# The opening of a fused attention kernel: load order, useless products and the second group's transposes

## Chip, cores and metric

The kernel runs on one core of a Trainium2 chip. The metric is the device time of the core in microseconds, from the start of the program to its end; before the change it is 969.23 us (median of 3 runs, 967.59 to 970.59).

## The reference

Six stages work on x, 16 batches of 128 tokens with 256 features in float32, each adding its result to x. Only the first, an attention with low-rank (LoRA) updates of its four weights, is touched:

```python
def lora_linear(x, W, b, Bm, Am):
    out = jnp.einsum('bld,od->blo', x, W) + b
    upd = jnp.einsum('blr,or->blo', jnp.einsum('bld,rd->blr', x, Bm), Am)
    return out + SCALING * upd           # rank 16, SCALING = 0.5
q = _split(lora_linear(x, Wq, bq, Bq, Aq))      # 16 heads of 16; k and v alike
scores = jnp.einsum('bhqd,bhkd->bhqk', q, k) * SCALE
attn = jax.nn.softmax(scores, axis=-1)
out = jnp.einsum('bhqk,bhkd->bhqd', attn, v)
return lora_linear(out, Wo, bo, Bo, Ao)
...
x = x + _L0_attn_ref(_layernorm(x, axis=-1), ...)
```

Then follow a causal convolution stage, a mixture of low-rank experts, a wide attention, a linear attention and a mixture of experts.

## The kernel before

Each engine has a program of its own, written out by hand, and the programs meet at semaphores. One function, lora_attention, gives the programs of the five engines for the first stage: sync_program (SP, which only issues transfers), gpsimd_program, tensor_program, scalar_program and vector_program. The order of the work on each engine is the order of the lines.

The 16 batches are worked in NG = 4 groups of G = 4. The unit of the attention loop (n, from 0 to 63) is four heads of one batch, so that a group has U = 16 units; g and u are group and unit (lines 533 and 534). In unit n TensorE transposes the probabilities (turn), makes the scores of units n + 4 and n + 5 on even n (scores), multiplies the values of unit n - 1 (weigh), and projects a batch now and then (project). Between these, `extra` puts the next group's input through its steps: transposes of the normalised input (turn_x, chunk 0 and 1, line 178), products for queries and keys (q_or_k) and values. Each large product is made of three with high and low parts of the operands (lines 50 to 52). ScalarE makes the high parts (hi_chunk, line 185), keeps the queries, keys and values that come out of PSUM (keep_q, keep_k, keep_v) and takes the exponentials (exps). VectorE makes the low parts (lo_chunk, line 189), row maxima (row_max), inverse sums, and the copies of the transposed probabilities (keep_probT), and the layer norm (vector_stats, vector_apply). GpSimd takes the power for the norm (line 173) and normalises the probabilities (line 332).

Ahead of the loop comes the opening. SP loads the LoRA factors (lines 300 and 301), x of the first group in two halves (303), the queries' weight (305) and the other three (306), waits for six transfers (`loaded`), and then loads x of the other groups and what later stages need. ScalarE issues five small transfers on its own queue: the unit matrix ident, then v_bias, out_bias, qk_bias and parity (559 to 563). TensorE waits for the factors (494), multiplies each weight's factors (503), then runs eight products whose result nobody reads (keep_busy, 498) on the factors' own tiles, waits for `loaded`, transposes the first group's input, runs three more useless products, and goes on with queries, keys, the bias product (521), the scores of units 0 to 3, the values, and the transposes of chunk 0 of group 1 (530). VectorE adds the factor products to the raw weights (fold, 726), ScalarE rounds them (637) and VectorE makes their low parts (low, 731); fold(0) and low(0) come first.

Of PSUM's banks, b_p[0] and b_p[1] serve the projections and transposes in turn, b_s[0] to b_s[3] the scores, b_t the transposed probabilities and the useless products. Scores of unit n + 4 go to the bank of unit n, so scores(4) waits until exps(1) is done (line 389).

## Time and profile before

| What | Value |
|---|---|
| Median of 3 runs | 969.23 us (967.59 to 970.59) |
| The profiled execution's own time | 968.73 us |
| Its span | 966.9 us |
| Mean granted TensorE clock | 0.998 |
| TensorE busy | 936.3 us, 97% |
| VectorE busy | 625.4 us, 65% |
| ScalarE busy | 476.9 us, 49% |
| GpSimd busy | 239.4 us, 25% |

All rows are of one profiled execution. The span runs from its first to its last instruction; the kernel's time has 1.8 us around it. In the rows PE is TensorE, PEld its weight loads, DVE VectorE, ACT ScalarE, POOL GpSimd, and SPq or ACTq the issue of a transfer by SP or ScalarE. L498 is line 498 of the kernel before. A float32 product is recorded as two passes, so that eight products are 16 records. The records of neighbouring passes overlap, because the engine takes up the next before the last one has drained: their pace is read from start to start, not from the duration of one. The raw weights and the factors lie in one buffer that a later stage uses too, and which is named w_or_y.

### The profile page before, as it was taken

To read this page: it belongs to the slowest core of one execution; us is meant where nothing else is said; L and a number is where in the kernel's file an instruction comes from. 1 tells how busy PE (TensorE), PEld (TensorE's weight loads), DVE (VectorE), ACT (ScalarE), POOL (GpSimd) and SP (SyncE) were. 2 spreads that over 40 slices of the span, in tenths; PEclk is the share of its full clock that TensorE was granted. 3 is DMA by queue.
4 is the path that set the end of the run, shared out by engine and by line. 5 is a ranking of instruction groups with operands and counts; after the bars stand their busy time and mean duration, and the time that the engine had idled before them with its cause. 6 is when DMAs were issued, how large, how long until landed. Compare 5 with 4: busy or idle time off the path is not lost.

```text
span 966.9 us, 20053 instructions
## 1 busy us (share of the span) xinstructions
PE 936.3 (97%) x7655; PEld 794.8 (82%) x7655; DVE 625.4 (65%) x1384; ACT 476.9 (49%) x1596; POOL 239.4 (25%) x258
## 2 busy tenths in 40 slices
PE   8999999999999999999999999999999999999888
PEld 6677777899788888888888888888888887677667
DVE  5778887897875575564456454546456665777864
ACT  4887876444445554444344444444444544444432
POOL 2555796672011111111111011111102212110010
PEclk9999999999999999999999999999999999999999
DMA  8100000002330000000000000010002004000002
GB/s 303 47 2 2 2 2 2 2 1 91 112 150 1 2 1 1 1 1 2 1 1 2 1 1 1 23 39 1 1 20 70 1 1 175 3 2 1 3 1 87
DMA packets 11325, 28.02 MB, mean 29 GB/s; under 512 B 1856, under 2 KB 7264, under 8 KB 10720
## 3 DMA queue, kind: packets, MB, share of 16 engines
q1 hardware_dynamic: 10512, 26.55, 7.7%
q8 instruction: 62, 1.02, 0.4%
q10 hardware_dynamic: 720, 0.20, 0.1%
q14 instruction: 31, 0.25, 0.1%
HBM read 24.65 MB, written 2.10 MB: 28 GB/s over the span
## 4 chain that ended last, share of the span: by engine, by line
PE 86%; DVE 7%; ACT 4%; issue 2%; POOL 0%; DMA 0%; SPq 0%; DVEq 0%; ACTq 0%
PE bank L50 15%; PE bank L52 14%; PE bank L51 14%; PE bank L2115 6%; PE bank L2064 5%; PE bank L395 3%; PE bank L405 3%; PE bank L2105 3%; PE bank L1979 2%; PE bank L1988 2%; PE bank L417 2%; PE bank L178 2%; PE bank L1062 2%; PE bank L1073 2%; PE bank L1564 1%
## 5 line engine op out<-in xcount | busy, mean ns | idle before, releaser
L1925 POOL TENSOR_TENSOR wa_prob<-wa_prob,wa_rsum 128x512 f32<-128x512 f32 x64 | 67.6, 1057 | 405.1 <-DVE wa_rsum L2498 405.1
L2297 ACT ACTIVATE wa_prob<-wa_prob,wa_negmax 128x128 f32<-128x128 f32 x256 | 99.8, 391 | 66.4 <-DVE wa_negmax L2487 66.1
L50 PE MATMUL bank<-norm_xT_hi,wide_hi 128*128 128x512 f32 x256 | 106.0, 414 | 0.2 <-DVE norm_xT_lo L189 0.2
L51 PE MATMUL bank<-norm_xT_lo,wide_hi 128*128 128x512 f32 x256 | 101.1, 395 | 0.0
L52 PE MATMUL bank<-norm_xT_hi,wide_lo 128*128 128x512 f32 x256 | 101.0, 395 | 0.0
L2554 DVE TENSOR_TENSOR wa_z_lo<-bank,wa_z_hi 128x512 fp32r<-128x512 f32 x64 | 44.3, 692 | 86.8 <-ACT wa_z_hi L2331 86.4
L592 ACT ACTIVATE v_prob<-bank,la_negmax 128x128 f32<-128x128 f32 x256 | 91.4, 401 | 2.0 <-DVE la_negmax L670 2.0
L2305 ACT COPY wa_q<-bank 128x512 f32<-128x512 f32 x64 | 37.6, 587 | 93.5 <-PE bank L52 93.5
L2312 ACT COPY wa_v<-bank 128x512 f32<-128x512 f32 x64 | 37.4, 585 | 89.5 <-PE bank L52 89.5
L332 POOL TENSOR_TENSOR v_prob<-v_prob,la_rsum 128x512 f32<-128x512 f32 x64 | 66.6, 1043 | 49.1 <-DVE la_rsum L675 49.0
L173 POOL TENSOR_TENSOR norm_rstd<-norm_rstd,minus_half 128x4 f32<-128x4 f32 x23 | 24.6, 1070 | 203.8 <-DVE norm_rstd L133 127.5
L2115 PEld LDWEIGHTS bank<-wa_probT,wa_v 128*128 128x128 f32 x512 | 65.4, 191 | 10.7 <-DVE wa_probT L2541 5.0
L50 PE MATMUL bank<-wide_hi,wa_z_hi 128*128 128x256 f32 x256 | 73.6, 288 | 0.3
L52 PE MATMUL bank<-wide_hi,wa_z_lo 128*128 128x256 f32 x256 | 72.4, 283 | 0.0
L51 PE MATMUL bank<-wide_lo,wa_z_hi 128*128 128x256 f32 x256 | 72.3, 282 | 0.0
L2115 PE MATMUL bank<-wa_probT,wa_v 128*128 128x128 f32 x512 | 68.3, 276 | 2.5 <-DVE wa_probT L2541 2.5
L2493 DVE COPY wa_k<-bank 128x512 f32<-128x512 f32 x64 | 44.3, 692 | 39.7 <-PE bank L52 39.7
L2541 DVE COPY wa_probT<-bank 128x512 f32<-128x512 f32 x64 | 44.0, 688 | 38.2 <-PE bank L2105 38.2
L2064 PE MATMUL bank<-wa_k,wa_q 128*128 128x128 f32 x512 | 67.6, 275 | 0.0
L2064 PEld LDWEIGHTS bank<-wa_k,wa_q 128*128 128x128 f32 x512 | 62.7, 192 | 0.4
L592 ACT ACTIVATION_READ_ACCUMULATOR v_prob<-bank,la_negmax 128x1 f32 x256 | 61.4, 240 | 0.0
L52 PEld LDWEIGHTS bank<-norm_xT_hi,wide_lo 128*128 128x128 f32 x256 | 48.0, 187 | 11.7
(275 smaller groups left out, 2379.3 us busy)
## 6 DMA issues: line engine op xcount, KB each, us to landing
wide_raw<-in_wide_w SPq DMA_DIRECT2D x16, 512.0 KB, 6.8
em_w<-in_em_w SPq DMA_DIRECT2D x1, 4096.0 KB, 13.3
lc_kt<-in_ctx_rev SPq DMA_DIRECT2D x1, 2048.0 KB, 10.7
lc_toep<-in_toeplitz SPq DMA_DIRECT2D x1, 2048.0 KB, 14.4
li_kt<-in_ctx_rev SPq DMA_DIRECT2D x4, 512.0 KB, 7.0
out_x<-x SPq DMA_DIRECT2D x8, 256.0 KB, 2.5
x<-in_x SPq DMA_DIRECT2D x3, 512.0 KB, 5.0
h_or_w<-in_li_w SPq DMA_DIRECT2D x1, 1024.0 KB, 5.1
```

The costliest lines, as they stand in the source:

```text
L50: nc.tensor.matmul(out, a[0], b[0], start=start, stop=False, skip_group_check=True)
L51: nc.tensor.matmul(out, a[0], b[1], start=False, stop=False, skip_group_check=True)
L52: return nc.tensor.matmul(out, a[1], b[0], start=False, stop=stop, skip_group_check=True)
L332: nc.gpsimd.tensor_tensor(own, own, rsum[:, n % NS, :].unsqueeze(2).to_broadcast([P, 4, P]), ALU.mult)\
L592: last = nc.scalar.activation(prob[:, n % NP, s, :], b_s[n % RG][:, s * P:(s + 1) * P], ACT.Exp, bias=negmax[:, n % NS, s:s + 1], accum_ou ...
L1925: nc.gpsimd.tensor_tensor(prob[:, s], prob[:, s], rsum[:, s, :].unsqueeze(2).to_broadcast([P, G, P]), ALU.mult).then_inc(prob_ok, 1)
L2064: last = nc.tensor.matmul(b_s[s][:, t], q[:, s, t], k[:, s, t], start=True, stop=True)
L2115: last = nc.tensor.matmul(b_z[:, j * P:(j + 1) * P], v[:, g % 2, j, m * HD:(m + 1) * HD], probT[:, h_ % 2, j, :], start=True, stop=True)
L2297: last = nc.scalar.activation(prob[:, s, j, :], prob[:, s, j, :], ACT.Exp, bias=negmax[:, s, j:j + 1], scale=SCALE, accum_out=sums[:, s, j ...
L2493: nc.vector.tensor_copy(k[:, s, :], b_p[1][:, :]).then_inc(k_ok, 1)
L2541: nc.vector.tensor_copy(probT[:, t % 2], b_t[:, :].rearrange("p (j k) -> p j k", j=G))\
L2554: nc.vector.tensor_tensor(z[1][:, t % 2, :], b_z[:, :], z[0][:, t % 2, :].bitcast(F32), ALU.subtract).then_inc(z_lo, 1)
```

## The change

All of it is in lora_attention.

- SP issues x of the first group first, then the queries' weight, the other weights and out_bias. ScalarE issues the two factors, ident, qk_bias, parity and v_bias. ident counts into `lora_loaded`, now three transfers, and `loaded` counts five.
- VectorE fills a tile of its own, idle, with ones. TensorE runs four useless products on it ahead of the wait for the factors; the eight and the three later ones read it too. TensorE's wait for `loaded` goes.
- q_bias is made on GpSimd, behind a wait for `loaded`.
- ScalarE rounds the values' and the output's weight (high(2), high(3)) between the keep_k's; exps(1) comes right behind exps(0), and keep_v of the second half comes in the loop, after exps(2).
- VectorE makes low(1) before fold(2), low(2) after the statistics of group 1, low(3) at the end of unit 1. The normalisation of group 1 is applied in two halves, the second at the end of unit 0.
- The transposes of group 1's chunk 0 move into unit 0 of the loop, those of chunk 1 from unit 0 to unit 1; the first query and key products of group 1 come one unit later (Q_AT, 2 for g = 0). The wait for all low parts moves from the loop's head to the first projection.

The diff, with the counts of semaphores at the kernel's end left out:

```diff
@@ lora_attention
+    idle = probT[:, 0, 0:2, :].rearrange("p s k -> p (s k)")
+    idle_ok = sem("idle_operand_ready")
-    NLOAD = 6
+    NLOAD = 5
+    Q_AT = [2] + [1] * (NG - 2)
@@ sync_program
-        sp.dma_start(lora_b[:], io["l0_b"]).then_inc(lora_loaded, 16)
-        sp.dma_start(lora_a[:], io["l0_a"]).then_inc(lora_loaded, 16)
         for sem_, first in ((pr.x_loaded[0], 0), (x_second, 2)):
...
         sp.dma_start(w_raw[:, 1:4], io["l0_w"][:, 1:4]).then_inc(loaded, 16)
+        sp.dma_start(out_bias[:], io["l0_o_bias"]).then_inc(loaded, 16)
@@ gpsimd_program
         norm.pool_rstd(pool, 0)
+        pool.wait_ge(loaded, 16 * NLOAD)
+        for e in range(2):
+            ins = nc.gpsimd.tensor_tensor(q_bias[:, e, :], qk_bias[:, 0, :], parity[:, e:e + 1].to_broadcast([P, DC]),
+                                          ALU.mult)
+        ins.then_inc(qb_ok, 1)
@@ tensor_program, project
+            if b == 0:
+                pe.wait_ge(w_lo, 4)
@@ tensor_program, extra
-            if u == 0:
-                if g == 0:
-                    pe.wait_ge(norm.s_lo, DC * norm.split(0) + 1)
-                else:
-                    pe.wait_ge(v_ok, 2 * g + 2)
+            if g == 0 and u == 0:
+                pe.wait_ge(v_ok, 1)
+                turn_x(1, 0, b_p[0])
+            elif g == 0 and u == 1:
+                pe.wait_ge(norm.s_lo, DC * norm.split(0) + 1)
+                turn_x(1, 1, b_p[0])
+            elif u == 0:
+                pe.wait_ge(v_ok, 2 * g + 2)
                 turn_x(t, 1, b_p[0])
-            elif u == 1:
+            elif u == Q_AT[g]:
                 pe.wait_ge(norm.s_lo, DC * norm.split(t))
                 q_or_k(t, 0, 0, b_p[0], q_ps)
-            elif u == 3:
+            elif u == Q_AT[g] + 2:
@@ tensor_program
-        pe.wait_ge(lora_loaded, 16 * 2)
-
         def keep_busy(count):
             for _ in range(count):
-                nc.tensor.matmul(b_t[:, 0:D], lora_b[:, 0:P], lora_a[:, :], start=True, stop=True)
+                nc.tensor.matmul(b_t[:, 0:D], idle[:, 0:P], idle[:, 0:D], start=True, stop=True)
+
+        pe.wait_ge(idle_ok, 1)
+        keep_busy(4)
+        pe.wait_ge(lora_loaded, 16 * 3)
...
         keep_busy(8)
-        pe.wait_ge(loaded, 16 * NLOAD)
...
         values(0, 1, b_p[1])
-        pe.wait_ge(v_ok, 1)
-        turn_x(1, 0, b_p[0])
-        pe.wait_ge(w_lo, 4)
         pe.wait_ge(bias_ok, 1)
@@ scalar_program
-        act.dma_start(pr.ident[:], io["ident"]).then_inc(loaded, 16)
-        act.dma_start(v_bias[:], io["l0_v_bias"]).then_inc(loaded, 16)
-        act.dma_start(out_bias[:], io["l0_o_bias"]).then_inc(loaded, 16)
+        act.dma_start(lora_b[:], io["l0_b"]).then_inc(lora_loaded, 16)
+        act.dma_start(lora_a[:], io["l0_a"]).then_inc(lora_loaded, 16)
+        act.dma_start(pr.ident[:], io["ident"]).then_inc(lora_loaded, 16)
         act.dma_start(qk_bias[:], io["l0_qk_bias"]).then_inc(loaded, 16)
         act.dma_start(parity[:], io["parity"]).then_inc(loaded, 16)
+        act.dma_start(v_bias[:], io["l0_v_bias"]).then_inc(loaded, 16)
@@ scalar_program, extra and extra_late
-            if u == 1:
+            if g == 0 and u == 1:
+                norm.hi_chunk(act, 1, 0, b_p[0], xT[1][0])
+            elif u == Q_AT[g]:
                 norm.hi_chunk(act, t, 1, b_p[0], xT[t % 2][0])
...
-            if u == 2:
+            if u == Q_AT[g] + 1:
                 keep_q(t, 0, b_p[0])
@@ scalar_program
-        for n in range(4):
+        def high(n):
             act.wait_ge(w_f32, n + 1)
             nc.scalar.copy(w[0][:, n], w_raw[:, n]).then_inc(w_hi, 1)
-            if n == 0:
-                for c in range(DC):
-                    norm.hi_chunk(act, 0, c, b_p[c], xT[0][0])
+
+        high(0)
+        for c in range(DC):
+            norm.hi_chunk(act, 0, c, b_p[c], xT[0][0])
+        high(1)
         act.wait_ge(qb_ok, 1)
-        for m in range(DC):
-            keep_q(0, m, b_p[m])
-        for m in range(DC):
-            keep_k(0, m, K_FIRST[m])
+        keep_q(0, 0, b_p[0])
+        keep_q(0, 1, b_p[1])
+        keep_k(0, 0, K_FIRST[0])
+        high(2)
+        keep_k(0, 1, K_FIRST[1])
+        high(3)
         exps(0)
+        exps(1)
         act.wait_ge(v_zero, 1)
         keep_v(0, 0, b_p[0])
-        keep_v(0, 1, b_p[1])
-        exps(1)
-        norm.hi_chunk(act, 1, 0, b_p[0], xT[1][0])
...
                 exps(n + 2)
+            if n == 0:
+                keep_v(0, 1, b_p[1])
@@ vector_program
+        nc.vector.memset(idle, 1.0).then_inc(idle_ok, 1)
         dve.wait_ge(pr.x_loaded[0], 16)
...
-        for e in range(2):
-            ins = nc.vector.tensor_scalar(q_bias[:, e, :], qk_bias[:, 0, :], parity[:, e:e + 1], None, ALU.mult)
-        ins.then_inc(qb_ok, 1)
+        low(1)
         fold(2)
-        low(1)
         fold(3)
-        low(2)
-        low(3)
         dve.wait_ge(pr.x_loaded[1], 16)
         norm.vector_stats(dve, 1)
+        low(2)
         row_max(0)
         row_max(1)
-        norm.vector_apply(dve, 1)
+        norm.vector_apply_half(dve, 1, 1, 0)
+        inverse_sums(0)
         dve.wait_ge(bias_ps, 1)
         nc.vector.tensor_tensor(out_bias[:], b_t[:, 0:D], out_bias[:], ALU.add).then_inc(bias_ok, 1)
-        inverse_sums(0)
         row_max(2)
-        norm.lo_chunk(dve, 1, 0, b_p[0], *xT[1])
@@ vector_program, in the loop
+            if n == 1:
+                norm.lo_chunk(dve, 1, 0, b_p[0], *xT[1])
-            if u == 1 and g + 1 < NG:
+            if g + 1 < NG and u == Q_AT[g]:
                 norm.lo_chunk(dve, g + 1, 1, b_p[0], *xT[(g + 1) % 2])
...
+            if n == 0:
+                norm.vector_apply_half(dve, 1, 1, 1)
+            if n == 1:
+                low(3)
```

## Rows read from the trace of the kernel before

**Rows 1.** The page: engine busy time and share; the chain that ended last, by engine.

```profile
PE 936.3 (97%) x7655; PEld 794.8 (82%) x7655; DVE 625.4 (65%) x1384; ACT 476.9 (49%) x1596; POOL 239.4 (25%) x258
...
PE 86%; DVE 7%; ACT 4%; issue 2%; POOL 0%; DMA 0%; SPq 0%; DVEq 0%; ACTq 0%
```

**Rows 2.** Busy time by stretch: start:end, length, each engine's busy us (instructions), clock, DMA.

```profile
40.00:60.00 20.00, 20.00 (x222) 15.16 (x220) 17.06 (x46) 17.06 (x84) 12.87 (x15) 1.00 0.01 1
```

**Rows 3.** Timeline of TensorE: start us, us, engine, line, operation, count [idle before <-releaser].

```profile
3.62 2.09 PE L503 MATMUL bank<-w_or_y 16*128 16x256 f32 x16 [3.62 <-DMA w_or_y<-in_l_a]
5.64 6.47 PE L498 MATMUL bank<-w_or_y 128*128 128x256 f32 x16
11.95 1.04 PE L178 MATMUL bank<-ident,norm_xn 128*128 128x128 f32 x8
12.82 1.46 PE L498 MATMUL bank<-w_or_y 128*128 128x256 f32 x6
14.54 0.50 PE L50 MATMUL bank<-norm_xT_hi,la_w_hi 128*128 128x512 f32 x1 [0.26 <-DVE norm_xT_lo L189]
...
21.26 1.72 PE L395 MATMUL bank<-la_k,la_q 32*128 32x128 f32 x32
...
26.68 0.63 PE L405 MATMUL bank<-ident,v_prob 128*128 128x128 f32 x4 [0.22 <-POOL v_prob L332]
28.26 1.16 PE L395 MATMUL bank<-la_k,la_q 32*128 32x128 f32 x16 [0.95 <-ACT v_prob L592]
...
30.72 0.63 PE L405 MATMUL bank<-ident,v_prob 128*128 128x128 f32 x4 [0.69 <-DVE v_prob L680]
...
31.89 0.50 PE L50 MATMUL bank<-la_xT_hi,la_w_hi 128*128 128x512 f32 x1 [0.18 <-DVE la_xT_lo L189]
...
35.00 0.43 PE L417 MATMUL bank<-v_prob 128*32 128x128 f32 x8
```

**Rows 4.** Timeline of VectorE.

```profile
7.55 0.06 DVE L144 MEMSET wait_slot<- 1x1 f32 x1
...
9.33 1.38 DVE L166 TENSOR_SCALAR norm_xn<-x,norm_meanvar,norm_rstd 128x256 f32<-128x256 f32 x4 [0.59 <-POOL norm_rstd L173]
...
24.92 0.42 DVE L761 TENSOR_TENSOR la_out_bias<-bank,la_out_bias 128x256 f32<-128x256 f32 x1
...
28.63 0.69 DVE L189 TENSOR_TENSOR la_xT_lo<-bank,la_xT_hi 128x512 fp32r<-128x512 f32 x1 [2.63 <-ACT la_xT_hi L185]
...
29.89 0.68 DVE L680 COPY v_prob<-bank 128x512 f32<-128x512 f32 x1
```

**Rows 5.** Line 498 alone, 11 to 12 us: duration min/median/max in ns, starts.

```profile
L498 PE MATMUL bank<-w_or_y x5: 379/380/634, 10.5 to 11.7; 128*128 128x256 f32 x5
```

**Rows 6.** Timeline of ScalarE.

```profile
26.06 0.65 ACT L584 COPY v_prob<-bank 128x256 f32<-128x256 f32 x2 [0.72 <-PE bank L52]
...
30.06 0.59 ACT L185 CAST la_xT_hi<-bank 128x512 fp32r<-128x512 f32 x1
```

**Rows 7.** DMA issues in the first 60 us: tiles, queue, size, us to landing.

```profile
x<-in_x SPq DMA_DIRECT2D x3, 512.0 KB, 5.0
w_or_y<-in_l_w SPq DMA_DIRECT2D x1, 768.0 KB, 6.5
x<-in_x SPq DMA_DIRECT2D x2, 256.0 KB, 4.5
...
w_or_y<-in_l_w SPq DMA_DIRECT2D x1, 256.0 KB, 5.2
...
w_or_y<-in_l_a SPq DMA_DIRECT2D x1, 128.0 KB, 2.4
...
ident<-in_ident ACTq DMA_DIRECT2D x1, 64.0 KB, 2.6
...
la_parity<-in_parity ACTq DMA_DIRECT2D x1, 1.0 KB, 5.3
```

**Rows 8.** Timeline of GpSimd.

```profile
8.27 1.02 POOL L173 TENSOR_TENSOR norm_rstd<-norm_rstd,minus_half 128x4 f32<-128x4 f32 x1 [4.00 <-DVE norm_rstd L149]
```

## What the change should do

> **What bounds the kernel now.** I read the page first. TensorE is busy 97% of the span and holds 86% of the chain that ended last [rows 1]. Time is therefore saved where TensorE stands idle, or where it does work that nobody needs. I then split the span into stretches. Between 40 and 60 us TensorE is never idle [rows 2], so the attention loop is bound by TensorE from there on, and its later waits are short ones on its own producers. A shift at the entry of the loop should arrive at the end nearly whole. All of the change lies ahead of that, in the first 36 us, which I read from the timelines engine by engine.
>
> There the reader is to see two stretches. The first is the opening. TensorE waits 3.62 us for the factors, multiplies them (2.09 us), and then works through the eight useless products of line 498, recorded as 16 passes of 256 columns. The input's transposes (line 178) start at 11.95 and the query products at 14.54 [rows 3]. But the normalised input was ready at 9.33 + 1.38 = 10.71 [rows 4]. So the useless products, and not the input, release the transposes: 11.95 - 10.71 = 1.24 us are lost to them. They are long because they run slowly: of the last five, which start between 10.5 and 11.7 us, the longest takes 634 ns and the middle one 380 ns [rows 5], and 16 passes need 11.95 - 5.64 = 6.31 us where six passes later need about 1.29 us from the end of the transposes at 12.99, or 0.215 us each [rows 3]. Sixteen at that pace are 3.44 us. The granted clock prints as 1.00 throughout, but a pace of one half against the other is the lower of the two levels (1.2 GHz) until about 11.0 and the higher (2.4 GHz) after it: the clock rose some 5.4 us after the first of the eight products and 7.4 us after the first factor product.
>
> The second stretch is the entry of the loop. TensorE idles 0.22 us before turn(0), 0.95 us before scores(4), 0.69 us before turn(1) and 0.18 us before the first query products of group 1, together 2.04 us [rows 3]. The longest follows from ScalarE's order: keep_v of the second half runs at 26.06 and puts exps(1) behind it [rows 6], and scores(4) may overwrite its bank only after exps(1).
>
> **The change part by part.**
>
> *Issue order.* The input's two transfers move from third and fourth on SP's queue to first and second. Each issue ahead of them takes about 0.45 us, so they are issued 0.93 us earlier. The factors move to ScalarE's queue, where ident follows them. They are issued at the same times as now, but ident, which was first there, is now third, at 1.66, and the wait before the factor products now includes it. v_bias goes to the end of ScalarE's six transfers and out_bias to the end of SP's. These small ones are read late (bias product, loop), so they cost nothing, and six issues end at some 3.65 us, ahead of ScalarE's first work. If both halves of x take as long to land as now (4.5 us), the normalised input comes 0.93 us earlier, at 9.8. If they land as the first factors do (2.4 us) [rows 7], the second half is there at 3.6 and the input could be ready at about 8. I take a point between, 9.3. The queries' weight is issued 0.97 us earlier and lands by 6.9 at the present 5.2 us, ahead of fold(0). The rest of the weights go from 9.66 to about 9.2; fold(1) then still ends before the first low chunk is due at 10.4, and x of group 1, 5.0 us behind, is there at 14.2 to 14.7, when VectorE has just finished fold(3).
>
> *Factors.* Two queues now work on 256 KB each at the same time, and ident is third. Its landing is bounded by 1.66 + 2.6 = 4.3 below and, by parity's 5.3 us, by 7.0 above [rows 7]. I take 4.5, since 64 KB behind 256 KB is near the factors' own case. That is 0.9 us later than the factor products start now. The Trainium skill, DMA: Bandwidth & Descriptors, section Queues, rings and completion order, says that an engine takes turns between the queues that have work for it. By that rule the factors no longer have the engines for themselves, which speaks against this edit. No row here shows two large transfers on two queues, so the sum goes by the bounds above.
>
> *Four more useless products.* VectorE's memset of the idle operand is no form that the trace shows on that engine. Its bounds are the one-element memset (0.06) and a 256-column operation with two inputs, 0.42 [rows 4]. With the issue at about 0.73 the products start at about 1.1. At the low clock eight passes of 0.425 take 3.4 us, until 4.5. They lie in time in which TensorE waits anyway, so their own cost is nothing unless the factors land before 4.5 (then up to 0.2 us). What they may give is an earlier clock. If it has risen when the factors come, the factor products take 1.05 instead of 2.09, and the eight products 3.44 instead of 6.31: 4.6 + 1.05 + 3.44 = 9.1. The transposes then go by the later of 9.1 and the input's 9.3, so by about 9.45 with the usual tenth between engines. That is 2.5 us ahead of 11.95.
>
> The Trainium skill, TensorE: Matmul & The Clock Gate, Part 1, says that the gate's timing is not tied to a kernel's start, so that the rise comes after different numbers of matmuls in different runs. By that rule neither the gain nor its absence would be the same in all runs. The trace is one execution and cannot show it.
>
> *Orders on VectorE, ScalarE and GpSimd before the loop.* q_bias moves to GpSimd: two 128x2 operations, each between nothing and the 1.02 us of its 128x4 power [rows 8], in an idle stretch between 9 and 13 us, ahead of keep_q. The power for group 1 is queued behind, but its variance comes later. VectorE loses two small operations there. high(2) and high(3) move behind the keep_q's and keep_k(0,0). ScalarE then starts keep_q as soon as the first query bank is done instead of at 17.11. keep_k(0,1) is still done within the 0.86 us of the bias product (one copy is 0.7), so scores(0) starts as now, 6.72 us behind the first query product (21.26 - 14.54). low(2) comes with 2 us to spare before the value products.
>
> *Entry of the loop.* Measured from the start of scores(0) (S), the value products end at S + 4.6. exps(0) ends at S + 3.4; with only half of the apply (0.7 us) in front of it on VectorE, inverse_sums(0) and the normalisation (1.04) give turn(0) at S + 4.85, an idle 0.25. exps(1) now follows exps(0) at once and ends at S + 4.95, so scores(4) has no wait: the 0.95 us is gone. What is late next is the second group's input. Its second half is applied on VectorE only after row_max(3) and keep_probT(0): from S + 5.8, 0.65 + 0.7 us [rows 4] give S + 7.15, where TensorE has been waiting since S + 6.55: 0.7 us. This new wait stands in front of turn(1). turn_x(1,1) then waits for hi (0.59, ScalarE) and lo (0.69, VectorE) of chunk 0, with turn(1) and weigh(0) (0.9 us) as cover: 0.6 us idle. The query products at u = 2 have scores(6) as cover, and I cost their wait at 0.05; with that cover gone it would be the present 0.18 or, with both copies uncovered, 1.3. Sum: 0.25 + 0.7 + 0.6 + 0.05 = 1.6 against 2.04, so 0.45 us gained, which I round to 0.5. The same work (up to weigh(1), at 35.36 now [rows 3]) is compared. low(3) runs in n = 1 and is needed by project(0) in n = 7, 10 us later.
>
> **Sum.** 2.5 + 0.5 = 3.0 us. Against the profiled execution's own 968.73 (span 966.9 and 1.8 around it) that is 965.7. The median of the three runs is 0.5 above that execution, so I forecast 966.2 (0.31% below 969.23). From the ends of the landing times this case holds 965.8 (the products bind, at 9.1) to 966.9 (the input at 9.8, or factors at 5.5).
>
> **The rivals.**
> 1. *The clock rises only in the eight products.* The first four are followed by the factor products, which use 16 rows in four groups. In the trace the clock stayed low through those and rose 5.4 us after the full-size products began. If the first four don't bring the rise, the present opening is only shifted: factors at 4.5, and 2.05 + 6.31 behind them gives 12.86, 0.9 later than now. With 0.5 gained in the loop that is +0.4, 969.6. If the clock rises in their first half, one to two microseconds come back: 967.5 to 969.6. For it: that order of events. Against: four full-size products, 3.4 us of work, now stand ahead.
> 2. *Slower: ident gates the factor products.* With the clock low the transposes start at L + 8.36, L being the last of the three landings; they are later than now from L = 3.6, and the kernel is slower from L = 4.1. At the top bound L = 7.0 it would be 3.4 - 0.5 = +2.9, 972.1; at a middling 5.5 it is 970.6. For it: ident is third on a queue that now shares the engines. Against: ident took 2.6 us, like the factors. It decides only if the clock stays low; at the high clock L may be 4.9 before the input is overtaken.
> 3. *The entry of the loop takes the gain back.* VectorE's order in n = 0 and n = 1 is longer, and each step of it that slips adds to TensorE. If the two new waits (1.3) come on top of all that is left of the present ones (2.04 - 0.95 = 1.09), the entry costs 0.35 more instead of 0.5 less, and with both copies uncovered another 1.3: 967.1 to 968.4.
> 4. *The change doesn't do what it says*: x lands no earlier because it shares with the factors, and input at 10.7 holds the transposes at 10.8. Then 1.15 + 0.5 = 1.65: 967.6.
>
> **How the numbers follow.** A measurement of this kernel can tell about 0.3% (2.9 us) from no change, and the forecast stands almost on that line. Chances: forecast 0.50, rival 1 0.25, rival 2 0.07, rival 3 0.10, rival 4 0.08. Faster by over 0.3% needs less than 966.3, which the forecast's case gives in about half of its span; with something for a base whose three runs lie 3 us apart, 0.33. Slower by over 0.3% is the upper end of rival 2 alone: 0.05. The rest is within: 0.62. The range goes down to 964.4 (input ready at 8 and the base's spread) and up through rivals 4, 3 and nearly all of 1, to 969.9. What is left out is rival 2 and the tails.
>
> **What would show it.** Right: passes of line 498 near 380 ns from the factor products on, transposes at 9.1 to 9.8, query products at about 12.0, scores(4) with no wait, two waits of 0.6 to 0.7 before the line 178 transposes of group 1, and weigh(1) ending some 3 us ahead of 35.36 in spite of its neighbours' new order. Wrong: passes of 634 ns through the eight products; ident landing after 5; a stall at scores(0), which would mean that keep_k(0,1) is late behind high(2); or idle time in the stretch of 40 to 60 us, which would mean that the shift is given back later.

## The result and the profile after

The changed kernel takes 971.43 us (median of 16 runs, 967.66 to 974.17) where the kernel before, beside it, takes 969.23 (16 runs, 967.59 to 971.25). The ratio is 1.0020, 95% interval 1.0012 to 1.0029: 2.2 us slower, a small loss that the measurement tells from none. The forecast was 966.2 with a range up to 969.9, so it was wrong in sign and in range. The profiled execution of the changed kernel took 970.75, 0.7 below its median, with a span of 969.0 us against 966.9.

The timeline of TensorE in the changed kernel answers to [rows 3] (start us, us, engine, line, operation, count, idle before and its releaser; line 508 holds the useless products, 517 the factor products, 402 the scores, 412 turn):

```profile
1.19 3.78 PE L508 MATMUL bank<-v_prob 128*128 128x256 f32 x8 [1.19 <-DVE v_prob L751]
6.08 2.09 PE L517 MATMUL bank<-w_or_y 16*128 16x256 f32 x16 [1.11 <-DMA ident<-in_ident]
8.10 6.49 PE L508 MATMUL bank<-v_prob 128*128 128x256 f32 x16
14.43 1.04 PE L178 MATMUL bank<-ident,norm_xn 128*128 128x128 f32 x8
...
23.76 1.72 PE L402 MATMUL bank<-la_k,la_q 32*128 32x128 f32 x32
...
30.77 0.63 PE L178 MATMUL bank<-ident,norm_xn 128*128 128x128 f32 x4 [0.43 <-DVE norm_xn L155]
...
32.80 0.66 PE L178 MATMUL bank<-ident,norm_xn 128*128 128x128 f32 x4 [0.61 <-DVE la_xT_lo L189]
...
38.46 0.63 PE L412 MATMUL bank<-ident,v_prob 128*128 128x128 f32 x4 [0.52 <-DVE v_prob L697]
```

The reader is to see that the factor products start 2.46 us later than before the change (6.08 against 3.62), released by ident and not by a factor, and that everything behind them is the old opening, shifted: 2.09 us for the factors, 6.33 us for the eight products, transposes at 14.43, 2.48 us late. The scores start 2.50 us late. In the loop's entry the idle times are 0.43 + 0.61 + 0.52 = 1.56 us where they were 2.04. Less of this arrives than the idle column says: at turn(16), the first of the second group, the changed kernel is 66.06 - 63.90 = 2.16 us late, so that the entry gives back 0.34 us and not 0.48. Before and after:

```profile
63.90 0.38 PE L405 MATMUL bank<-ident,v_prob 128*128 128x128 f32 x2
```

```profile
66.06 0.49 PE L412 MATMUL bank<-ident,v_prob 128*128 128x128 f32 x3
```

At 910 us the difference is 2.28. The spans differ by 2.1 only, because the execution before lost some 0.2 us that the changed one did not: its granted clock fell at 915 to 919 us, where the changed kernel's reads 1.00. Busy time by stretch, before (the clock is the third number from the end):

```profile
914.00:916.00 2.00, 0.74 (x6) 0.54 (x3) 1.97 (x5) 0.24 (x1) 0.28 (x1) 0.94 0.00 0
916.00:918.00 2.00, 2.00 (x23) 1.27 (x25) 2.00 (x4) 0.00 (x0) 0.00 (x0) 0.50 0.01 4
918.00:920.00 2.00, 2.00 (x38) 1.41 (x32) 1.78 (x7) 0.79 (x4) 0.53 (x1) 0.70 0.04 8
```

Such a late fall stands in some of the traces below and not in others (e4 and e8 lose some 0.8 us by theirs), so that differences of a few tenths between two spans say nothing of the opening. The loss is in the opening alone.

The DMA issues of the first 60 us (tile, queue, KB, us from issue to landing), which answer to [rows 7]:

```profile
x<-in_x SPq DMA_DIRECT2D x2, 256.0 KB, 4.3
w_or_y<-in_l_w SPq DMA_DIRECT2D x1, 256.0 KB, 5.4
w_or_y<-in_l_b ACTq DMA_DIRECT2D x1, 128.0 KB, 3.4
w_or_y<-in_l_a ACTq DMA_DIRECT2D x1, 128.0 KB, 3.9
...
ident<-in_ident ACTq DMA_DIRECT2D x1, 64.0 KB, 4.4
```

The factors take 3.4 and 3.9 us instead of 2.5 and 2.4, and ident 4.4 instead of 2.6. The Trainium skill, DMA: Bandwidth & Descriptors, section Queues, rings and completion order, has the engines take turns between queues with work. The rows agree as far as the factors take 0.9 and 1.5 us longer beside the input than they took with their queue's start to themselves; the input itself, now first, took 4.3 instead of 4.5.

The input, for whose sake the order was changed, was indeed ready earlier. Timeline of VectorE (751 fills the idle tile, 743 is the fold, 166 the apply), against [rows 4]:

```profile
0.86 0.27 DVE L751 MEMSET v_prob<- 128x256 f32 x1 [0.86 <-PEq L2800]
...
8.32 0.69 DVE L743 SCALAR_TENSOR_TENSOR w_or_y<-bank,w_or_y 128x512 f32<-128x512 f32 x1 [1.08 <-PE bank L517]
8.93 1.37 DVE L166 TENSOR_SCALAR norm_xn<-x,norm_meanvar,norm_rstd 128x256 f32<-128x256 f32 x4
```

It is ready at 10.30 instead of 10.71, after a wait of 1.08 us: the apply stands behind fold(0), and fold(0) waits for the late factor products. TensorE did not take it up until 14.43. Line 508's passes say why the eight products are long here too (duration min/median/max in ns, starts, 13 to 13.5 us):

```profile
L508 PE MATMUL bank<-v_prob x3: 561/634/634, 12.5 to 13.4; 128*128 128x256 f32 x3
```

The clock was at its lower level until about 13.6, 5.5 us after the first of the eight, as in [rows 5]. The four new products ahead of the factors ran at that level and did not bring the rise in this execution.

### The profile page after: what moved, and what is told of

The parts are those of the page before. It is cut to its first block, busy times and chain, and to the rows that moved or that the text cites. A ratio compares the mean times of both kernels' runs of the same rounds, so it can differ in the third digit from the quotient of the medians.

```text
span 969.0 us, 20069 instructions
## 1 busy us (share of the span) xinstructions
PE 938.7 (97%) x7663; PEld 796.5 (82%) x7663; DVE 625.5 (65%) x1383; ACT 476.9 (49%) x1596; POOL 240.4 (25%) x260
## 4 chain that ended last, share of the span: by engine, by line
PE 85%; DVE 8%; ACT 4%; issue 2%; DMA 0%; POOL 0%; ACTq 0%; DVEq 0%
PE bank L50 15%; PE bank L52 14%; PE bank L51 14%; PE bank L2134 6%; PE bank L2083 5%; PE bank L402 3%; PE bank L412 3%; PE bank L2124 3%; PE bank L1998 2%; PE bank L2007 2%; PE bank L178 2%; PE bank L424 2%; PE bank L1583 1%; PE bank L1081 1%; PE bank L1092 1%
## 6 DMA issues: line engine op xcount, KB each, us to landing
em_w<-in_em_w SPq DMA_DIRECT2D x1, 4096.0 KB, 13.5
lc_kt<-in_ctx_rev SPq DMA_DIRECT2D x1, 2048.0 KB, 11.2
```

## The experiments

Each variant was timed beside the kernel before on the same chip, where that had 969.1 to 969.2. All variants start from the changed kernel, unless it is said. The semaphore counts at the kernel's end and the value of NLOAD (6 where `loaded` has the old six transfers) are left out of the edits, and so are variants' lines that another edit shown here has. Times are medians, and ratios are to the kernel before, with their 95% intervals. e1 to e12 stand for the labels that begin so.

### Ident apart from the factors (e2_ident_apart)

```diff
@@ scalar_program
-        act.dma_start(pr.ident[:], io["ident"]).then_inc(lora_loaded, 16)
+        act.dma_start(pr.ident[:], io["ident"]).then_inc(loaded, 16)
@@ tensor_program
-        pe.wait_ge(lora_loaded, 16 * 3)
+        pe.wait_ge(lora_loaded, 16 * 2)
...
         keep_busy(8)
+        pe.wait_ge(loaded, 16 * NLOAD)
```

> The changed kernel, but ident counts into the weights' semaphore again, and TensorE waits for that ahead of the transposes: the factor products wait for the factors alone. These landed at 1.19 + 3.9 = 5.1, ident at 6.1. If everything behind is a pure shift (sum L + 8.35), the transposes start at 13.45 instead of 14.43 and the kernel gains 1.0 us on the changed one. If the gap of 1.1 us was what cost the clock, 0.1 us of gap may let it rise early, at 6.7 to 8.7: transposes at 10 to 11.5, 3 us or more gained.

Measured: 967.66 us (11 runs, 966.05 to 970.56), ratio to before 0.9984 (0.9974 to 0.9994), so 3.8 us faster than the changed kernel. This one wait was worth more than the whole loss. It is also more than the 1.0 us expected from the changed kernel's trace. In the profiled execution, the slowest of the 11 (970.56), the factors landed at 5.95 after a pause of 0.98 us and the clock stayed low; ident took 6.1 us from its issue, and would have held the factor products until 7.8. So this trace shows a slow execution; what the other ten do, and with it how the 3.8 us divide between the wait and the clock, no trace shows.

### Filling the pause (e1_fill_gap)

```diff
-        keep_busy(4)
+        keep_busy(6)
         pe.wait_ge(lora_loaded, 16 * 3)
```

> The changed kernel with six useless products ahead of the factors instead of four, so that the 1.11 us in which TensorE waited for ident are filled (1.19 + 12 passes of 0.425 us = 6.3). Theory A, an idle gap is what undoes the first products: the clock rises 5.5 us after 1.19, or 7.5 us after it, so at 6.7 to 8.7 and no longer at 13.6; the transposes start at 11.2 to 12.2 instead of 14.43 and the kernel is 2.2 to 3.2 us faster than the changed one. Rival B, the factor products (16 rows in four groups) do not carry the clock and break the run as well: the rise stays 5.5 us behind the start of the eight, now 8.4, transposes at 14.7, 0.2 us slower than the changed kernel.

Measured: 969.55 us (967.57 to 973.20), ratio 1.0003 (0.9991 to 1.0014). Timeline of TensorE:

```profile
1.18 4.46 PE L508 MATMUL bank<-v_prob 128*128 128x256 f32 x12 [1.18 <-DVE v_prob L751]
8.73 2.09 PE L517 MATMUL bank<-w_or_y 16*128 16x256 f32 x16 [3.08 <-DMA ident<-in_ident]
10.75 5.66 PE L508 MATMUL bank<-v_prob 128*128 128x256 f32 x16
```

Twelve passes at the low level take 5.1 us; here they took 4.46 with the tail of the last one, so the clock rose inside them. Then ident landed only at 8.6, TensorE stood idle for 3.08 us, and the factor products took 2.09 us again: the clock had fallen. Neither theory comes out as written. The pause was not filled, because ident's landing moves by more than the pause.

### The old queues under the changed kernel (e5_old_queues)

The transfers are issued in the order and on the queues of before the change, and ident counts with the weights; the four products stay.

```diff
@@ sync_program
+        sp.dma_start(lora_b[:], io["l0_b"]).then_inc(lora_loaded, 16)
+        sp.dma_start(lora_a[:], io["l0_a"]).then_inc(lora_loaded, 16)
...
-        sp.dma_start(out_bias[:], io["l0_o_bias"]).then_inc(loaded, 16)
@@ scalar_program
-        act.dma_start(lora_b[:], io["l0_b"]).then_inc(lora_loaded, 16)
-        act.dma_start(lora_a[:], io["l0_a"]).then_inc(lora_loaded, 16)
-        act.dma_start(pr.ident[:], io["ident"]).then_inc(lora_loaded, 16)
+        act.dma_start(pr.ident[:], io["ident"]).then_inc(loaded, 16)
+        act.dma_start(v_bias[:], io["l0_v_bias"]).then_inc(loaded, 16)
+        act.dma_start(out_bias[:], io["l0_o_bias"]).then_inc(loaded, 16)
...
-        act.dma_start(v_bias[:], io["l0_v_bias"]).then_inc(loaded, 16)
@@ tensor_program
-        pe.wait_ge(lora_loaded, 16 * 3)
+        pe.wait_ge(lora_loaded, 16 * 2)
...
         keep_busy(8)
+        pe.wait_ge(loaded, 16 * NLOAD)
```

> The changed kernel with the transfers issued as before the change (factors first on SP, ident on ScalarE), but still with the four useless products ahead. The factors land at 3.6, inside the four products (to 4.97 on the changed kernel), so there is no idle gap. Theory A (a gap undoes them): the clock rises at 6.7 to 8.7; factor products from 5.0 to about 7, transposes at 10.8 (input ready at 10.7), 1.1 us earlier than before; with the entry's 0.5 it is 1.6 us faster than before. Rival B (the factor products do not carry the clock): transposes at 5.0 + 8.35 = 13.3, 0.9 us slower than before.

Measured: 967.37 us (966.89 to 968.53), ratio 0.9980 (0.9971 to 0.9989). Theory A's number was 967.6. Timeline:

```profile
1.18 3.78 PE L509 MATMUL bank<-v_prob 128*128 128x256 f32 x8 [1.18 <-DVE v_prob L752]
4.90 1.65 PE L518 MATMUL bank<-w_or_y 16*128 16x256 f32 x16
6.47 3.72 PE L509 MATMUL bank<-v_prob 128*128 128x256 f32 x16
11.14 1.06 PE L178 MATMUL bank<-ident,norm_xn 128*128 128x128 f32 x8 [0.95 <-DVE norm_xn L166]
```

With no pause the clock rises inside the factor products (1.65 us, between the 2.09 of the low level and 1.15 below), the record of the eight is 3.72 us long, and TensorE is ahead of the input by 0.95 us. The four products do what they are for, if the factors are there when they end.

### The loop's entry alone (e4_entry_only)

As the last one, without the four products:

```diff
-        keep_busy(4)
```

> The loop's entry and the orders ahead of it as changed, but the transfers' queues and waits as before the change and no products ahead of the factors. The transposes start at 11.95 as before the change. The traces of the two kernels give 2.04 us of TensorE idle at the entry before and 0.43 + 0.61 + 0.52 = 1.56 after, so 0.5 us faster than the kernel before (0.05%). If the entry is what made the change slow, this kernel is 2 us slower than before.

Measured: 967.93 us (967.10 to 968.26), ratio 0.9985 (0.9976 to 0.9994). The kernel is 1.2 us faster than before and not 0.5, and the runs lie within 1.2 us of each other where the kernel before scatters over 3.2 beside it. Its profiled execution (968.02) gains 0.3 us at the entry, as the changed kernel's does, so the larger part of the 1.2 comes from elsewhere. The next run shows where it may come from.

### The operand of the useless products (e6_ones_operand)

The kernel before with one edit:

```diff
-                nc.tensor.matmul(b_t[:, 0:D], lora_b[:, 0:P], lora_a[:, :], start=True, stop=True)
+                nc.tensor.matmul(b_t[:, 0:D], idle[:, 0:P], idle[:, 0:D], start=True, stop=True)
```

> The kernel before with one edit: the useless products read a tile of ones that VectorE fills, instead of the factors (half of whose rows are zeros). The kernel that had the entry alone came out 1.24 us faster than before, where its traces account for 0.35 us at the entry; its clock rose at about 9.3 instead of 11.2. Theory C, the operand's data decide when the clock rises: this kernel is 0.8 to 1.0 us faster than before. Rival, chance of the execution: no difference (within 0.3 us), and the spread of the runs stays.

Measured: 969.38 us (968.70 to 971.10), ratio 1.0006 (0.9997 to 1.0015). The operand's data bring no gain: the median is 0.3 us above that of before, within what the runs can tell, where theory C had 0.8 to 1.0 below. But its trace shows the entry of the old loop with a fall of the clock. Timeline, and busy time by stretch (the clock is the third number from the end):

```profile
27.35 1.16 PE L397 MATMUL bank<-la_k,la_q 32*128 32x128 f32 x16 [0.95 <-ACT v_prob L595]
28.46 0.65 PE L178 MATMUL bank<-ident,norm_xn 128*128 128x128 f32 x4
29.81 1.09 PE L407 MATMUL bank<-ident,v_prob 128*128 128x128 f32 x4 [0.69 <-DVE v_prob L683]
...
32.00 0.63 PE L51 MATMUL bank<-la_xT_lo,la_w_hi 128*128 128x512 f32 x1
...
33.20 0.39 PE L51 MATMUL bank<-la_xT_lo,la_w_hi 128*128 128x512 f32 x1
```

```profile
28.00:30.00 2.00, 1.30 (x15) 0.96 (x12) 2.00 (x6) 1.94 (x11) 1.22 (x2) 0.92 0.05 18
30.00:32.00 2.00, 2.00 (x13) 1.20 (x13) 1.99 (x5) 2.00 (x13) 1.77 (x3) 0.50 0.02 4
32.00:34.00 2.00, 2.00 (x10) 1.64 (x8) 0.29 (x1) 0.73 (x5) 1.51 (x2) 0.73 0.02 4
```

After the waits of 0.95 and 0.69 us the granted clock goes to 0.50, the lower of the two levels, and comes back near 33.1. The kernel before has the same two waits and no fall in [rows 3]; the trace of e7, whose entry is the old one too, has the fall (granted clock 0.50 from 38 to 40 us, behind the same two waits). turn takes 1.09 instead of 0.63, and a 512-column product 0.63 instead of 0.39. From the scores' start to weigh(1) this execution needs 35.28 - 20.35 = 14.93 us, where [rows 3] have 35.00 - 21.26 = 13.74: 1.19 us lost.

The times of the kernel before are of two kinds. Of its 110 on record, 81 lie between 967.5 and 969.5, 29 between 970.0 and 971.3, and none between. Where the mean granted clock is on record (94 of them), it is 0.994 to 0.996 for the slower kind and 0.997 to 1.000 for the other, so the slower executions had the lower clock for longer. At which place in the kernel is not on record. One fall at the entry is not enough for the slower kind: the profiled execution above, with its fall, is the fastest of its eleven (968.70), since its transposes started at 11.01 where those of [rows 3] started at 11.95. And the kernel before's profiled execution (968.73) has a fall too, the late one. For the entry as the place speak that e4 and e5 have no run of the slower kind and no mean clock below 0.997, and that two of three profiles with the old entry show a fall there and none of the eleven with the new one. That the fewer falls at the entry are the larger part of e4's 1.2 us is likely by this, and not shown.

### The queues alone (e7_queues_only)

The kernel before with the changed transfers and the wait for all three, and nothing else:

```diff
@@ sync_program
-        sp.dma_start(lora_b[:], io["l0_b"]).then_inc(lora_loaded, 16)
-        sp.dma_start(lora_a[:], io["l0_a"]).then_inc(lora_loaded, 16)
...
+        sp.dma_start(out_bias[:], io["l0_o_bias"]).then_inc(loaded, 16)
@@ scalar_program
-        act.dma_start(pr.ident[:], io["ident"]).then_inc(loaded, 16)
-        act.dma_start(v_bias[:], io["l0_v_bias"]).then_inc(loaded, 16)
-        act.dma_start(out_bias[:], io["l0_o_bias"]).then_inc(loaded, 16)
+        act.dma_start(lora_b[:], io["l0_b"]).then_inc(lora_loaded, 16)
+        act.dma_start(lora_a[:], io["l0_a"]).then_inc(lora_loaded, 16)
+        act.dma_start(pr.ident[:], io["ident"]).then_inc(lora_loaded, 16)
...
+        act.dma_start(v_bias[:], io["l0_v_bias"]).then_inc(loaded, 16)
@@ tensor_program
-        pe.wait_ge(lora_loaded, 16 * 2)
+        pe.wait_ge(lora_loaded, 16 * 3)
```

> The kernel before with the changed transfers alone: input first on SP, factors and ident on ScalarE's queue, the factor products waiting for all three. In the changed kernel ident landed at 6.08, in two other kernels with the same queues at 7.8 and 8.6. With the shift of L + 8.35 from L = 3.62 the kernel is 2.5 us slower than before in the first case (971.7) and up to 5 us in the last (974). If instead the loop's entry or the four products made the change slow, it is within 0.5 us of before.

Measured: 975.11 us (5 runs, 973.95 to 976.13), ratio 1.0058 (1.0045 to 1.0070). The waits of TensorE (line waited for, us, times, longest) and the issues:

```profile
PE bank L502 <- DMA ident<-in_ident: 9.9, 1, 9.9
```

```profile
w_or_y<-in_l_a ACTq DMA_DIRECT2D x1, 128.0 KB, 4.3
...
ident<-in_ident ACTq DMA_DIRECT2D x1, 64.0 KB, 8.1
```

This part alone costs 6 us. Ident's 64 KB took 8.1 us, and the factor products started at 9.90, 6.3 us later than before. The transposes start at 17.75, 5.8 us late, and the fall of the clock at the old entry adds 1.3 us in this execution.

### Without the four products (e3_no_first)

```diff
-        keep_busy(4)
```

> The changed kernel without the four products ahead of the factors; all else as changed. If the pause until ident lands undoes them (theory A), leaving them out changes nothing: within 0.5 us of the changed kernel, 971.4. If they do help the clock in some executions, the median is up to 1 us above the changed kernel's.

Measured: 972.59 us (6 runs, 972.16 to 972.75), ratio 1.0033 (1.0021 to 1.0045). The median is 1.2 us above the changed kernel's, and the six runs lie within 0.6 us where the changed kernel's lie within 6.5: with the four products some executions are fast, without them none of six is. How much of the 1.2 us is theirs is not shown, since ident landed at 8.8 in this trace and at 6.08 in the changed kernel's. This trace also accounts for e7, which has neither the four products nor the new entry and is 2.5 us slower. After the entry the two traces are 3.0 us apart: ident is 1.1 us later in e7, the clock rises 0.3 us later behind it, the old entry costs 0.3, and its fall of the clock 1.3.

### A late start without the shared queues (e8_late_start)

The old queues and the four products, with one more wait ahead of the factor products:

```diff
+        pe.wait_ge(pr.x_loaded[0], 16)
```

> The changed kernel with the transfers issued as before the change, in which the factor products also wait for the first half of x (at 6.1 to 6.4) though the factors are there at 3.6. It makes the pause of the changed kernel (some 1.3 us behind the four products) without the shared queues. If the pause and the late start are the whole cost, the transposes start at 6.2 + 8.35 = 14.5 and it is as slow as the changed kernel, 971 to 971.5, against 967.37 without the wait. If contention on the queues costs besides, it is clearly faster than the changed kernel. If the four products keep the clock in spite of the pause, it stays at 968.

Measured: 969.62 us (967.24 to 970.82), ratio 0.9997 (0.9986 to 1.0007), so 2.2 us slower than without the wait. Timeline of the profiled execution (968.21):

```profile
1.19 3.78 PE L509 MATMUL bank<-v_prob 128*128 128x256 f32 x8 [1.19 <-DVE v_prob L753]
6.39 1.15 PE L519 MATMUL bank<-w_or_y 16*128 16x256 f32 x16 [1.43 <-DMA x<-in_x]
7.46 3.72 PE L509 MATMUL bank<-v_prob 128*128 128x256 f32 x16
11.08 1.06 PE L178 MATMUL bank<-ident,norm_xn 128*128 128x128 f32 x8
```

Here a pause of 1.43 us did not stop the rise: the factor products ran at the full level (1.15). Five of the twelve runs lie within 967.2 and 968.3, the others between 969.2 and 970.9. The two kinds of times suggest that after four products and a pause the clock is up in some executions and not in others; in the changed kernel's profiled one it was not. Waiting alone accounts for 2.2 of the 4.1 us between the changed kernel and the old queues. The other 1.9 are not settled. The two traces don't show ident coming later than x: it released the factor products at 6.08 in the changed kernel, x at 6.39 here. But other traces with the changed queues have ident at 7.8 to 9.9, so that later landings in some of the executions would explain it.

### The order on ScalarE's queue (e12_ident_first)

```diff
+        act.dma_start(pr.ident[:], io["ident"]).then_inc(lora_loaded, 16)
         act.dma_start(lora_b[:], io["l0_b"]).then_inc(lora_loaded, 16)
         act.dma_start(lora_a[:], io["l0_a"]).then_inc(lora_loaded, 16)
-        act.dma_start(pr.ident[:], io["ident"]).then_inc(lora_loaded, 16)
```

> The changed kernel with ident issued first on ScalarE's queue, ahead of the factors; the factor products still wait for all three. If what costs is ident's third place behind 256 KB on a queue that shares the engines (it landed at 6.1 to 9.9 in four traces), ident now lands at about 3.5 and the factors, second and third, at 5.3 to 6.2: the kernel is close to that with ident apart, 967.7 to 968.7. If whatever is third is late in the same way, the second factor lands at 6 to 9 and the kernel stays at 971.

Measured: 970.00 us (966.49 to 972.90), ratio 1.0013 (1.0000 to 1.0026). The issues in the profiled execution, the slowest of the twelve:

```profile
w_or_y<-in_l_b ACTq DMA_DIRECT2D x1, 128.0 KB, 3.7
w_or_y<-in_l_a ACTq DMA_DIRECT2D x1, 128.0 KB, 6.7
...
ident<-in_ident ACTq DMA_DIRECT2D x1, 64.0 KB, 3.0
```

Now ident lands in 3.0 us and the second factor in 6.7: in this trace it is the third place that is late, whatever stands there. TensorE waited 3.58 us for it. The median lies between the two expectations.

### Six and eight, six and four, four and five products (e9, e10, e11)

e9 is e2 with six products ahead of the factors, e10 the same with four instead of eight behind them. e11 is e5 with five instead of eight behind. The edits to e2 (e9 and e10) and to e5 (e11):

```diff
@@ e9
-        keep_busy(4)
+        keep_busy(6)
@@ e10
-        keep_busy(4)
+        keep_busy(6)
...
-        keep_busy(8)
+        keep_busy(4)
@@ e11
-        keep_busy(8)
+        keep_busy(5)
```

> The kernel with ident apart (967.66) and six instead of four products ahead of the factors. There TensorE paused 0.98 us between the four and the landing of the factors. If filling that pause makes the early rise of the clock surer, the runs narrow to their fast end and the median falls to 966.5 to 967. If the clock rises by chance of the execution, pause or none, the median stays at 967.7 and up to 0.4 us is added where the factors land before 6.3.

Measured: 967.52 us (967.13 to 968.41), ratio 0.9987 (0.9978 to 0.9996). The median is e2's and not the 966.5 to 967 that was expected of a filled pause, but the scatter shrinks from 4.5 to 1.3 us. Both ends went: no run is above 968.41, and none is as fast as e2's fastest five (966.05 to 967.07). Without a pause the eleven runs show no late rise.

```profile
1.19 5.35 PE L508 MATMUL bank<-v_prob 128*128 128x256 f32 x12 [1.19 <-DVE v_prob L752]
6.46 1.15 PE L517 MATMUL bank<-w_or_y 16*128 16x256 f32 x16
...
11.27 1.09 PE L178 MATMUL bank<-ident,norm_xn 128*128 128x128 f32 x8
```

> As the last one, with four instead of eight products behind the factors. The input is ready at 10.2 with these queues. With the clock risen by the factors, the eight end at 6.3 + 1.05 + 3.44 = 10.8 and four at 9.1, so up to 0.6 us is gained; with a late clock the eight end at 14 and four at 11.7, 2 us gained there, but the clock may then rise during the transposes or the query products, which costs up to half of that. Expected 966.2 to 966.9, the fastest so far.

Measured: 967.25 us (966.14 to 968.97), ratio 0.9980 (0.9971 to 0.9989). The forecast was 966.2 to 966.9. In its profiled execution (968.97, the slowest of the eleven) TensorE waited before the transposes, and they ran slowly:

```profile
11.24 1.97 PE L178 MATMUL bank<-ident,norm_xn 128*128 128x128 f32 x8 [2.65 <-DMA la_v_bias<-in_l_v_bias]
```

The transfer that releases them, v_bias, is the sixth on ScalarE's queue and lands at 11.2. TensorE waits for it at this place because e2's edit puts the wait for `loaded` back. In e9's trace the eight products hide that landing, in this one four don't, and the clock fell in the wait (1.97 us for what takes 1.04).

> The kernel with the old queues and four products ahead (967.37), with five instead of eight products behind the factors. In its trace TensorE waited 0.95 us for the input at 11.14, so with an early clock nothing changes; with a late one the five end at 7.0 + 4.25 = 11.2 instead of 13. Expected 967.0 to 967.3 and no run above 968. If it is slower than 967.8, the shorter run of products lets the clock rise later, inside the query products.

Measured: 968.23 us (967.43 to 968.89), ratio 0.9990 (0.9981 to 0.9998), 0.9 us slower than e5 and above the 967.8 at which the expectation called itself wrong.

```profile
11.40 1.24 PE L178 MATMUL bank<-ident,norm_xn 128*128 128x128 f32 x8 [2.82 <-DVE norm_xn L166]
12.44 2.77 PE L509 MATMUL bank<-v_prob 128*128 128x256 f32 x6
```

Three products fewer leave a wait of 2.82 us for the input, and the clock falls inside the transposes: six passes take 2.77 us where they took 1.46. Products that nobody reads are worth their time as long as TensorE would otherwise stand idle.

The fastest kernels (e10, e5, e9) are 1.7 to 1.9 us faster than before and about 4 us faster than the changed one. Their order among themselves is within the scatter.

## Why the prediction was wrong

**The bound of the kernel** was read rightly. A shift at the entry of the loop arrives nearly unchanged as long as the clock is the same: 2.16 us at turn(16), 2.28 at 910 us. The 2.1 of the span has the late fall of the clock before the change in it.

**The landing of ident** is the step that failed first. The text took 4.5, near the factors' own case, from bounds of 4.3 and 7.0. It landed at 6.08 in the changed kernel's trace and at 7.8, 8.6, 8.8 and 9.9 in e2, e1, e3 and e7, beyond the upper bound in those four. The row that was taken as nearest, the factors', is of transfers that were first and second on their queue. A nearer row was in the trace of before and in no group of rows: out_bias, 128 KB, third on ScalarE's queue with the factors and the input on the other.

```profile
la_out_bias<-in_l_o_bias ACTq DMA_DIRECT2D x1, 128.0 KB, 3.9
```

Issued at the same 1.66, it landed at 5.6, from where on rival 2's formula has the kernel 1.5 us slower. The text says that no row shows two large transfers on two queues. That holds for the rows that it picked, not for the trace. The edit's cost was then hidden in a single number, the count of the wait (two transfers to three): e2 shows that this one wait, with what it does to the clock, costs 3.8 us.

**The clock.** The forecast needed it to have risen by the factor products. In the changed kernel it had not, and the eight took their 6.3 us. In size this is the larger part. The transposes were forecast at 9.45 and came at 14.43, 4.98 us later: ident accounts for 1.5, the low clock under the factor products and the eight for 3.9 (2.02 and 6.33 us where the sum had 1.05 and 3.44), less the 0.36 that was left for the input. That products ahead of the factors can bring the rise was right: e5 (four) and e9 (six) have it, with transposes at 11.1 and 11.3. That it depends on the landing was said only in one direction ("unless the factors land before 4.5"); that a pause behind the four products puts the rise at risk was not in the sum.

That late ident makes the pause and the pause keeps the clock low, so that the two failures are one, is likely and not shown. Of the traces with products ahead of the factors, the two in which the clock had not risen by the end of the factor products have pauses of 1.11 and 0.98 us (the changed kernel and e2); those with none or hardly any (e5, e9, e10, e11) all have the rise. But e8 has it with 1.43, and e1 and e12 had it before their long waits and lost it there. The cited rule of the Trainium skill (TensorE: Matmul & The Clock Gate, Part 1), by which the rise is not tied to a kernel's start, agrees with the runs. The same opening but for the operand took 6.31 us for the eight products before the change and 5.21 in e6. Twelve passes ahead of the factors took 4.46 and 4.41 us in e1 and e10, where the clock rose inside them, and 5.35 in e9, where it did not until their end.

**Rival 2** named what happened, ident gating the factor products under a low clock, and its formula meets the changed kernel's trace to 0.01 us: 6.08 + 8.36 = 14.44 against 14.43. That closeness is luck. The distance from the factor products to the transposes depends on when the clock rises: it is 8.11 us in e2, 7.85 in e7, 7.5 to 7.8 in e1, e3 and e12, and 7.15 and 7.23 in e4 and e6. It was given 7 in 100, for the sake of ident's old 2.6 us. Rival 1, with L = 4.5, has the same formula. Together they had 32 in 100, on the wrong side of the evidence: nothing in [rows 7] showed a third transfer on a loaded queue landing soon.

**The input** was forecast ready at 9.3 and was ready at 10.30. Its landing took 4.3 us, near the 4.5 of before, and fold(0), ahead of the apply on VectorE, waited 1.08 us for the factor products. That chain, factors to fold to apply, was not in the text, and it makes early input useless as long as the factors are late: in e1 the apply started only at 11.58.

**The weights and the small transfers** were costed at nothing. That holds for the changed kernel, under the cover of the eight products; e10 shows the price once the cover is thinner and TensorE waits for `loaded` again, a wait of 2.65 us for v_bias.

**q_bias on GpSimd** held: its row (1.12 us for both at 9.83) is inside the bounds and released nobody.

**The loop's entry** was forecast at 1.6 us of idle time against 2.04, and is 1.56. The idle total is right with three of its terms off, and 0.34 us of the forecast 0.5 arrive behind the entry. The first new wait is 0.43 (forecast 0.7), the second 0.61 (0.6), the 0.25 before turn(0) is 0.12 by the starts and not in the idle column, and there is a wait of 0.52 before turn(4) that the text has not: with the key products moved from unit 3 to unit 4, turn(4) follows weigh(2) with no cover for keep_probT(3). And the old waits can cost more than their idle time: in e6 and e7 the clock fell behind them, for 1.2 and 1.3 us. How often, and how much of e4's 1.2 us this is, is not shown.

**The chances**: 0.05 for slower by over 0.3% and 0.62 for within; the measured +0.2% is within, but the time is 1.5 us above the range. The range took in ident's 4.5 and not its own upper bound.

What stays open is why ident's landing differs between 6.1 and 9.9 us from trace to trace with the same transfers, each kernel having only one trace, and what decides when the clock rises.

## What to carry to other kernels

A wait that counts one more transfer ends with the last of them, and its place in the queue sets the price: take its landing from the row of a transfer in the same place with the same traffic beside it, not from the same transfer when it was first. When two large streams are put on two queues, what stands third on either is the thing to ask for. Useless products paid while they covered a wait, and a wait left uncovered could cost the clock behind it besides its length (e10, e11), so that removing waits may give back more than the idle column shows.

## What was not expected of the hardware

- A 64 KB transfer took 2.4 to 2.7 us when first on its queue, 3.0 when first beside the input on the other, and 4.4 to 8.1 us when third, behind 256 KB and beside the input and the weights on the other queue. The 128 KB factor took 6.7 in the same place.
- The clock fell to half in the loop after waits of 0.95 and 0.69 us within 3.5 us (e6, granted clock 0.50 from 30 to 32 us, and e7, 0.50 from 38 to 40), though not after the same waits in the profiled execution of before, and in the opening after waits of 2.65 and 2.82 us (e10, e11) and 3.08 us (e1). After a wait of 1.43 us (e8) it was high.
- The printed granted clock doesn't show the low level ahead of the first change on record: it reads 1.00 in the opening of the changed kernel, where passes take 634 ns. The duration of equal passes shows it.
- The clock falls near the end of the kernel too, in some executions (before: 0.50 from 916 to 918 us) and not in others (the changed kernel: 1.00 throughout).
